# Joint wide and narrow attention: another filling order, another order of the last steps, and unit-matrix multiplications in the last four

## The chip, the core and the metric

The kernel runs on one core of a Trainium2 chip. The metric is the device time of one execution in microseconds, the median of three runs. A core has TensorE (PE: matrix products; its weight loads are shown as PEld), VectorE (DVE), ScalarE (ACT), GpSimd (POOL) and SyncE (SP), whose queue issues the DMAs here. Each engine takes its instructions in the order in which they were written and waits on semaphores.

## The reference

All of it is float32, on x of 32 batches, 128 tokens and 128 features, with a context of 128 tokens and 96 features for each batch. Five attention layers and two feed-forward layers follow one another; the change touches only the last two attention layers, which the kernel computes in one joint stage.

```python
# wide layer (L2): 16 heads of 64
h = layernorm(x, gamma, beta)
Q, K, V = h @ Wq, context @ Wk, context @ Wv          # 1024 columns each
attn = softmax(einsum('bihd,bjhd->bhij', Q, K), -1) * 64 ** -0.5
x = x + einsum('bhij,bjhd->bihd', attn, V).reshape(B, N, 1024) @ Wo + bo
# narrow layer (L3): 16 heads of 8, weights transposed in use
q, k, v = x @ Wq.T, context @ Wk.T, context @ Wv.T    # 128 columns each
attn = softmax(einsum('bhqd,bhkd->bhqk', q, k) * 8 ** -0.5, -1)
x = einsum('bhqk,bhkd->bhqd', attn, v).reshape(B, N, 128) @ Wo.T + bo + x
```

## The kernel before

The whole program is a row of stages with a barrier of all engines between them. The last stage, `wide_and_narrow`, starts at 1104.2 us of the profiled span and runs to its end. It is a software pipeline over the 32 batches: step t works on several batches at once, and each engine has its own list of what it does in a step (the loops `for t in range(first, last + 1)`, at the end of each engine's part). Steps run from -4 to 35. Operations of the wide layer begin with `w_`, those of the narrow one with `n_`.

The wide layer of batch b: statistics and mean (`w_statistics`, VectorE), one over the deviation and the normalised rows (`w_inverse_deviation`, `w_normalise`, GpSimd), a transposition (`w_transpose_h`, TensorE), scale and shift (`w_turned_h`, VectorE), queries in two halves (`w_queries`, eight instructions each), keys and values of two batches at a time in four quarters (`w_keys`, `w_values`; copied out by ScalarE, one quarter by VectorE), scores in two halves of eight heads (`w_score`), row maxima (VectorE), exponentials (ScalarE), sums, division (`w_divide`, GpSimd), and the turning of the probabilities in squares (`w_turn_squares`, VectorE) with two DMAs through device memory (`away`, `back`, on SP's queue). In step t TensorE makes the scores of batch t+1 first and weighs the values of batch t-1 after them. Until the first weighing, in step 1, most operations have nothing beside them: this is the filling, steps -4 to 0.

The narrow layer of batch b comes one step behind the wide one: transposition of x and projections in step b+1, then `n_set_parts` (GpSimd: six operations that lay keys and queries apart by groups of heads, so that four groups can use four row tiles of TensorE), scores whose maxima are taken (`n_score_for_max`, step b+2), the maxima turned and appended to the queries (`n_transpose_maxima`, `n_append_maxima`), scores less the maxima (`n_score_less_max`, step b+3, four groups in the order 2, 3, 0, 1), exponentials of each group, weighing (`n_weigh`, step b+4), turning back, division (`n_divide`), transposition (`n_transpose_o`), projection out and the sum with x (`n_finish`). After step 31 only the narrow layer is left but for the weighing of the last wide batch in step 32: in step 33 batch 31 has its scores for the maxima and batch 29 its weighing, in step 35 batch 31 its weighing and end.

PSUM has eight banks. Four hold scores: `scores[:, 0]` the wide scores' first half and the narrow scores for the maxima (`s_bank`), `scores[:, 1]` the second half and the narrow scores less the maxima (`t_bank`), two banks each, so groups 0 and 1 reuse the banks of groups 2 and 3. The other four are a ring that all other products go through; `Fills` lists them in the order of TensorE, and `start_fill` waits until the fill four places back was copied out.

`keep_clock` multiplies the unit matrix by itself a number of times; each is two instructions. The stage begins with ten of them.

Of the kernel before, what the change touches and what calls it, by code (L numbers as in the profile page):

```python
# [26 lines left out]
START_COUNT = 10  # L27
# [1287 lines left out]
def wide_and_narrow(nc, W, N, x, ctxT, ctx_blocks, ident, minus_half, eps, quad_mask, waits, store):  # L1315
# [8 lines left out]
             ("n.v", -3, "act"), ("n.Wo", -4, "dve"), ("n.mT", -2, "dve")]  # L1324
    first, last = -4, BATCHES + 3
    LAST_WIDE = BATCHES - 1
# [14 lines left out]
    def values_made(b):  # L1341
        return (b + 1) // 2 * 2 - 1

    ring = Fills((name, t + lag, engine) for t in range(first, last + 1)
                 for name, lag, engine in (turned_by_pe if t == LAST_WIDE + 1 else []) + order
                 if (makes_keys_values(t) if name.startswith("w.kv") else 0 <= t + lag < BATCHES))
    chunks = INNER // 128
# [9 lines left out]
    with ExitStack() as ctx:  # L1357
# [100 lines left out]

        def t_bank(g):
            return scores[:, 1, g % 2, :, :]  # L1460

        @block.tensor
        def _(pe):
            keep_clock(nc, scores[:, 0, 0, 0, :], ident, START_COUNT)
            for semaphore, value in waits:
# [8 lines left out]
            def filled_by(instruction, name):  # L1474
                instruction.then_inc(filled[ring.engine[name]], 1)

            def w_score(b, s):
# [37 lines left out]
            def n_score_less_max(b, g, j):  # L1515
                part = slice(QUAD * g, QUAD * (g + 1))
                if j == 0:
                    await_emptied(pe, "n.mT", b)
                    if g < 2:
                        pe.wait_ge(n_exp_ready, 4 * b + g + 1)  # L1520
                    elif real(b + 4):
                        pe.wait_ge(w_shifted, b + 5)
                    elif b >= 1:
                        pe.wait_ge(n_exp_ready, 4 * b - 3 + g)
                last = nc.tensor.matmul(t_bank(g)[:, j, :], n_k_apart[part, b % 2, j, :],  # L1525
                                        n_q_part[part, b % 2, j // 2, :],
                                        start=True, stop=True, tile_position=(QUAD * g, 0))
                if j == GROUP - 1:
                    last.then_inc(n_t_full, 1)
# [88 lines left out]

            def n_transpose_maxima(b):
                pe.wait_ge(n_max_ready, 4 * b + 4)  # L1620
                filled_by(nc.tensor.transpose(start_fill("n.mT", b)[:, 0:TOKENS],
                                              n_maxima[:, b % 2, :, :, :].rearrange("p g j d -> p (g j d)"),
                                              ident[:, :]), "n.mT")

            def n_weigh(b):
                pe.wait_ge(n_exp_ready, 4 * b + 4)
# [12 lines left out]

            def n_turn_back(b):  # L1640
                await_emptied(pe, "n.PV", b)
# [9 lines left out]

            def n_transpose_o(b):
                await_emptied(pe, "n.D", b)
                filled_by(nc.tensor.transpose(start_fill("n.oT", b)[:, 0:TOKENS],
                                              n_rows_o[:, :, :].rearrange("p h d -> p (h d)"), ident[:, :]), "n.oT")
# [12 lines left out]

            def n_project_out(b):
                await_emptied(pe, "n.oT", b)  # L1670
                filled_by(nc.tensor.matmul(start_fill("n.Wo", b)[:, 0:DIM], n_oT[:, :], N.wo[:, :],
                                           start=True, stop=True), "n.Wo")

            for t in range(first, last + 1):
                if t == LAST_WIDE + 1:
# [12 lines left out]
                if real(t - 1):  # L1688
                    w_project_out(t - 1)
                if real(t - 4):  # L1690
                    n_turn_back(t - 4)
                n_both_scores(t, (0, 1), (2, 3))
                if makes_keys_values(t):
                    if t % 2:
                        w_values(t)
                    else:
                        w_keys(t)
                n_both_scores(t, (2, 3), (0, 1))
                if real(t - 1):
# [17 lines left out]
        def _(act):  # L1717
# [25 lines left out]
            def n_exponentiate(b, g):  # L1743
                act.wait_ge(n_t_full, 4 * b + T_ORDER.index(g) + 1)
                nc.scalar.activation(n_exps[:, b % 2, GROUP * g:GROUP * (g + 1), :].rearrange("p h q -> p (h q)"),  # L1745
                                     t_bank(g).rearrange("p j q -> p (j q)"), ACT.Exp,
                                     scale=N.scale).then_inc(n_exp_ready, 1)
# [22 lines left out]
            def n_values(b):  # L1770
                if b == 0:
                    act.wait_ge(cleared, 3)
                copied("n.v", b, n_v[:, b % 2, :, :, 0:NARROW],
                       bank("n.v", b)[:, 0:DIM].rearrange("p (c e d) -> p c e d", e=2, d=NARROW))

            for t in range(first, last + 1):
                if t == LAST_WIDE + 1:
# [37 lines left out]
        def _(dve):  # L1815
            for semaphore, value in waits:
                dve.wait_ge(semaphore, value)
            nc.vector.memset(n_maxima[:, :, :, :, :], 0.0).then_inc(cleared, 1)
            nc.vector.memset(n_v[:, :, :, :, :], 0.0).then_inc(cleared, 1)
            dve.wait_ge(cleared, 2)  # L1820
            nc.vector.memset(n_v[:, :, :, :, NARROW:NARROW + 1], 1.0).then_inc(cleared, 1)

# [3 lines left out]
            def w_statistics(b):  # L1826
# [5 lines left out]
                nc.vector.memset(wait_carrier[:, :], 0.0)  # L1832
                nc.vector.bn_aggr(moments[:, p, :], stats[:, p, :]).then_inc(moments_ready, 1)

            def w_row_maxima(b, s):
# [58 lines left out]
            def n_append_maxima(b):  # L1894
# [5 lines left out]
                                               n_q_part[:, b % 2, 1, :], ALU.mult, ALU.add).then_inc(emptied["dve"], 1)  # L1900

            def n_divide(b):
                await_filled(dve, "n.D", b)
# [7 lines left out]
            def n_finish(b):  # L1911
# [3 lines left out]
                                        ALU.add).then_inc(emptied["dve"], 1)  # L1915

            for t in range(first, last + 1):
                if real(t + 1):
# [14 lines left out]
                if real(t - 1):  # L1933
                    w_finish(t - 1)
                if real(t - 4):
                    n_divide(t - 4)
                if real(t - 2):
                    n_find_maxima(t - 2, 0)
                    n_find_maxima(t - 2, 1)
                if real(t + 1) and t + 1 != LAST_WIDE:  # L1940
                    w_turn_squares(t + 1, 0)
# [9 lines left out]
                if real(t - 2):  # L1951
                    n_append_maxima(t - 2)

        @block.gpsimd
        def _(pool):
# [3 lines left out]
            def w_inverse_deviation(b):  # L1959
                p = b % 2  # L1960
                pool.wait_ge(moments_ready, b + 1)
                nc.gpsimd.tensor_tensor(var_eps[:, p, :], moments[:, p, 1:2], eps[:, :], ALU.add).then_inc(var_ready, 1)
                pool.wait_ge(var_ready, b + 1)
                nc.gpsimd.tensor_tensor(rstd[:, p, :], var_eps[:, p, :], minus_half[:, :],
                                        ALU.pow).then_inc(rstd_ready, 1)
# [27 lines left out]
            def n_set_parts(b):  # L1993
# [10 lines left out]
                done.then_inc(n_parts_ready, 1)  # L2004

            nc.gpsimd.memset(no_bias[:, :], 0.0).then_inc(masks_ready, 1)
            for n in range(2):
                nc.gpsimd.tensor_tensor(half_mask[:, n:n + 1], quad_mask[:, 2 * n:2 * n + 1],
                                        quad_mask[:, 2 * n + 1:2 * n + 2], ALU.add).then_inc(masks_ready, 1)
            pool.wait_ge(masks_ready, 3)  # L2010
            for t in range(first, last + 1):
                if real(t - 2):
                    n_set_parts(t - 2)
# [14 lines left out]
        def _(sp):  # L2028
# [10 lines left out]
            def back(b, h):  # L2039
# [4 lines left out]
                for j in range(SQUARES):  # L2044
                    sp.dma_start(w_probsT[SQUARE * j:SQUARE * (j + 1), b % 2, :, SLOT_HEADS * h:SLOT_HEADS * (h + 1), :],
                                 w_relay[h].rearrange("(i b) j h a -> j b i h a", b=SQUARE)[j]
                                 ).then_inc(w_probsT_landed[b % 2][h], 16)

            for t in range(first, last + 2):
                if real(t - 5):  # L2050
# [321 lines left out]
```

## Time and profile before

| | |
|---|---|
| runs | 1671.55 us median of 3 (1671.17 to 1672.45) |
| profiled execution: its time, its span | 1667.4 us, 1665.6 us |
| granted TensorE clock, mean over the span | 0.983 |
| busy over the span | PE 1599.6 us (96%), DVE 1201.9 (72%), ACT 1046.6 (63%), POOL 756.7 (45%) |
| joint stage | from 1104.2 us to the end |
| PE busy in 1120 to 1160 | 29.2 of 40 us |
| PE busy in 1202 to 1258 | 55.5 of 56 us |

The table is read so: in the middle of the stage TensorE hardly pauses, in its first 60 us it does. The granted clock is a share of full speed: 1.00 is 2.4 GHz, 0.50 is 1.2 GHz.

### The profile page before, as it was taken

What the parts mean: (1) busy time and instruction counts of PE and PEld (TensorE: products, weight loads), DVE (VectorE), ACT (ScalarE), POOL (GpSimd) and SP (SyncE); (2) the same over time, 40 slices, a digit from 0 to 9 for tenths busy, and PEclk for the clock granted to TensorE, in tenths of its full rate; (3) what the DMA queues carried; (4) which work ended last, traced back from release to release, by engine and by line L of the source; (5) the groups of instructions that cost most, each with busy time, mean ns of one, the idle gap of its engine ahead of it and who ended that gap; (6) DMA issues with size and microseconds to landing.
All of it is one profiled execution on the core that took longest, in us unless ns stands there. A gap on an engine that the chain in (4) does not pass through costs nothing. (4 is left out here: it accounts for less than half of the span.)

```text
span 1665.6 us, 49749 instructions
## 1 busy us (share of the span) xinstructions
PE 1599.6 (96%) x18240; PEld 1365.4 (82%) x18240; DVE 1201.9 (72%) x2395; ACT 1046.6 (63%) x3075; POOL 756.7 (45%) x1126
## 2 busy tenths in 40 slices
PE   7999999999999999989999998978999999999997
PEld 6888888878888888868978887867898898898986
DVE  5777777777777777746757775646887787888872
ACT  4777777777777777743336665435666666666663
POOL 3444444454444444422314442644555554555541
PEclk9999999999999999999999999998999999999997
DMA  7777667788677767740040000004545446444430
GB/s 198 197 196 188 184 184 200 201 210 217 185 187 192 188 185 192 190 140 9 0 115 2 3 3 2 1 1 127 154 137 166 145 136 178 124 141 146 135 117 9
DMA packets 229002, 220.07 MB, mean 132 GB/s; under 512 B 20610, under 2 KB 225092, under 8 KB 228740
## 3 DMA queue, kind: packets, MB, share of 16 engines
q1 hardware_dynamic: 228836, 217.79, 47.5%
q8 instruction: 112, 1.84, 0.5%
q14 instruction: 54, 0.44, 0.1%
HBM read 116.01 MB, written 101.71 MB: 131 GB/s over the span
## 5 line engine op out<-in xcount | busy, mean ns | idle before, releaser
L952 POOL TENSOR_TENSOR L_probs<-L_probs,L_inv_sum 128x1024 f32<-128x1024 f32 x128 | 242.8, 1897 | 88.3 <-DVE L_inv_sum L848 88.3
L736 ACT ACTIVATE L_probs<-L_scores,L_neg_max 128x128 f32<-128x128 f32 x512 | 182.7, 386 | 134.6 <-DVE L_neg_max L828 134.6
L822 DVE TENSOR_REDUCE L_row_max<-L_scores 128x8 f32<-128x1024 f32 x128 | 156.2, 1220 | 42.5 <-PE L_scores L594 42.5
L854 DVE STREAM_TRANSPOSE L_squares<-L_probs 128x1024 f32<-128x1024 f32 x125 | 153.0, 1224 | 0.3 <-POOL L_probs L952 0.3
L1983 POOL TENSOR_TENSOR L2L_w_probs<-L2L_w_probs,L2L_w_inv_sum 128x1024 f32<-128x1024 f32 x64 | 121.4, 1896 | 62.0 <-DVE L2L_w_inv_sum L1863 60.4
L1999 POOL TENSOR_SCALAR L2L_n_k_apart<-L2L_n_qk,quad_mask 128x128 f32<-128x128 f32 x128 | 55.5, 448 | 186.1 <-ACT L2L_n_qk L1724 175.8
L1735 ACT ACTIVATE L2L_w_probs<-L2L_scores,L2L_w_neg_max 128x128 f32<-128x128 f32 x256 | 91.2, 385 | 74.3 <-DVE L2L_w_neg_max L1843 74.3
L594 PE MATMUL L_scores<-L_kT,L_qT 64*128 64x128 f32 x2048 | 131.8, 278 | 0.9 <-ACT L_kT L725 0.9
L645 PE MATMUL L_ring<-L_probsT,L_v 128*64 128x128 f32 x2048 | 126.6, 276 | 4.7 <-issue 3.8
L645 PEld LDWEIGHTS L_ring<-L_probsT,L_v 128*64 128x64 f32 x2048 | 110.5, 137 | 24.7 <-issue 21.8
L594 PEld LDWEIGHTS L_scores<-L_kT,L_qT 64*128 64x128 f32 x2048 | 119.4, 188 | 12.5 <-ACT L_oT L725 8.1
L838 DVE TENSOR_REDUCE L_sums<-L_probs 128x8 f32<-128x1024 f32 x64 | 78.1, 1220 | 65.9 <-ACT L_probs L743 65.9
L1244 DVE TENSOR_REDUCE L_maxima<-L_s_banks 128x4 f32<-128x512 f32 x128 | 87.5, 688 | 43.5 <-PE L_s_banks L1066 43.5
L736 ACT ACTIVATION_READ_ACCUMULATOR L_probs<-L_scores,L_neg_max 128x1 f32 x512 | 115.7, 226 | 0.0
L725 ACT ACTIVATE L_oT<-L_ring 128x512 f32<-128x512 f32 x128 | 76.5, 599 | 40.5 <-PE L_ring L645 40.5
L1837 DVE TENSOR_REDUCE L2L_w_row_max<-L2L_scores 128x8 f32<-128x1024 f32 x64 | 76.8, 1199 | 28.6 <-PE L2L_scores L1494 28.6
L1745 ACT ACTIVATE L2L_n_exps<-L2L_scores 128x512 f32<-128x512 f32 x128 | 73.6, 605 | 37.8 <-PE L2L_scores L1525 37.7
L1891 DVE TENSOR_REDUCE L2L_n_maxima<-L2L_scores 128x4 f32<-128x512 f32 x128 | 82.3, 685 | 18.3 <-PE L2L_scores L1509 18.3
L1302 POOL TENSOR_SCALAR L_k_apart<-L_qk,quad_mask 128x128 f32<-128x128 f32 x116 | 50.3, 448 | 93.0 <-ACT L_qk L1202 93.0
L725 ACT ACTIVATE L_kT<-L_ring 128x512 f32<-128x512 f32 x128 | 76.8, 600 | 18.2 <-PE L_ring L602 18.2
L725 ACT ACTIVATE L_qT<-L_ring 128x512 f32<-128x512 f32 x128 | 76.2, 595 | 14.9 <-PE L_ring L602 9.5
L938 POOL TENSOR_TENSOR L_x_bias<-x,bias_L0a 128x128 f32<-128x128 f32 x32 | 14.6, 455 | 148.6 <-DVE x L870 148.6
(239 smaller groups left out, 4491.7 us busy)
## 6 DMA issues: line engine op xcount, KB each, us to landing
L_relay<-L_squares SPq DMA_DIRECT2D x125, 512.0 KB, 3.4
L_probsT<-L_relay SPq DMA_DIRECT2D x500, 128.0 KB, 3.7
L2L_relay<-L2L_w_squares SPq DMA_DIRECT2D x62, 512.0 KB, 3.6
L2L_w_probsT<-L2L_relay SPq DMA_DIRECT2D x248, 128.0 KB, 2.9
ctx_blocks<-ctx_turned SPq DMA_DIRECT2D x48, 128.0 KB, 3.5
out_x<-x SPq DMA_DIRECT2D x32, 64.0 KB, 2.8
ctx_turned<-ctxT SPq DMA_DIRECT2D x1, 1536.0 KB, 7.1
L0a_wq<-in_L_xattn_Wq SPq DMA_DIRECT2D x2, 256.0 KB, 3.1
```

The source lines that it names most:

```text
L594: last = nc.tensor.matmul(scores[:, s, r, i, :], q[part, i, at.n % 2, :], k[part, i, at.n % 2, :], start=True, stop=True, tile_position=(h ...
L645: last = nc.tensor.matmul(to[WIDE * r:WIDE * (r + 1), TOKENS * i:TOKENS * (i + 1)], v[:, at.n % 2, WIDE * h:WIDE * (h + 1)], probsT[:, at. ...
L725: nc.scalar.activation(to, src, ACT.Copy).then_inc(emptied["act"], 1)
L736: done = nc.scalar.activation(slot_probs(at, 0)[:, n, :], scores[:, 0, r, i, :], ACT.Exp, scale=layer_of(at).scale, bias=neg_max[:, n:n + ...
L822: nc.vector.tensor_reduce(row_max[:, s, :], slot(s), AX.X, ALU.max).then_inc(max_ready[s], 1)
L838: nc.vector.tensor_reduce(sums[:, :, 1, :], slot_probs(at, 1).rearrange("p (r i) k -> p r i k", r=2), AX.X, ALU.add).then_inc(sum_ready, 1)
L854: nc.vector.transpose(squares[:, at.n % 2, :, SLOT_HEADS * s:SLOT_HEADS * (s + 1), :] .rearrange("p j h a -> p h j a"), slot_probs(at, s). ...
L952: nc.gpsimd.tensor_tensor(to, to, inv_sum[:, :, s, :].unsqueeze(3) .to_broadcast([TOKENS, 2, GROUP, TOKENS]), ALU.mult).then_inc(divided, 1)
L1244: nc.vector.tensor_reduce(maxima[:, b % 2, g, :, 0:1].rearrange("p j d -> p (j d)"), s_bank(b, g), AX.X, ALU.max, negate=True).then_inc(ma ...
L1735: done = nc.scalar.activation(w_slot(b, 0)[:, h, :], scores[:, 0, r, i, :], ACT.Exp, scale=W.scale, bias=w_neg_max[:, h:h + 1], accum_out= ...
L1891: nc.vector.tensor_reduce(n_maxima[:, b % 2, g, :, 0:1].rearrange("p j d -> p (j d)"), s_bank(g), AX.X, ALU.max, negate=True).then_inc(n_m ...
L1983: nc.gpsimd.tensor_tensor(to, to, w_inv_sum[:, :, s, :].unsqueeze(3) .to_broadcast([TOKENS, 2, GROUP, TOKENS]), ALU.mult).then_inc(w_divid ...
```

## The change

The steps -4 to -1 are replaced by one written-out order on each engine, and the loops start at step 0. TensorE begins with the keys of batches 0 and 1, without the ten unit-matrix multiplications before; then it turns h of batches 0 and 1, makes the queries of batch 0, its scores, the queries of batch 1, turns h of batch 2 and makes the values of batch 0. The first three batches are normalised by VectorE, not GpSimd. VectorE's clearing of `n_maxima` and `n_v` (three memsets) moves from the stage's start to just before step 0. SP has the relay of batch 0's first half ahead of its loop. GpSimd's masks come after its first three deviations.

At the end: in step 32 VectorE, not GpSimd, sets the parts of batch 31, after it has appended the maxima of batch 30. In step 33 turning back batch 29 comes between the two blocks of scores, and its division after the maxima of the first two groups. In step 34 the scores less the maxima of batch 31 are made in one block of four groups, groups 0 and 1 in the banks of `scores[:, 0]`, and turning back batch 30 comes after them. In steps 33 to 35 `hold_clock` puts unit-matrix multiplications into a ring bank just before it is filled: 4, 3, 5 in step 33; 2, 3 in step 34; 4, 2, 3, 2 in step 35.

```diff
--- before.py
+++ after.py
@@ wide_and_narrow: fills of the ring, first step
-    first, last = -4, BATCHES + 3
+    first, last = 0, BATCHES + 3
+    DVE_NORMALISES = 3
+    kv = [(f"w.kv{g}", "dve" if g == 1 else "act") for g in QUARTERS]
+    filled_before = [*((name, -2, engine) for name, engine in kv), ("w.hT", 0, "dve"), ("w.hT", 1, "dve"),
+                     ("w.q0", 0, "act"), ("w.q1", 0, "act"), ("w.q0", 1, "act"), ("w.q1", 1, "act"),
+                     ("w.hT", 2, "dve"), *((name, -1, engine) for name, engine in kv)]
...
-        def t_bank(g):
-            return scores[:, 1, g % 2, :, :]
+        def t_bank(b, g):
+            return scores[:, 0 if b == BATCHES - 1 and g < 2 else 1, g % 2, :, :]
@@ TensorE
-            keep_clock(nc, scores[:, 0, 0, 0, :], ident, START_COUNT)
...
+            def hold_clock(name, b, count):
+
+                if b > LAST_WIDE - 3:
+                    keep_clock(nc, start_fill(name, b)[:, 0:TOKENS], ident, count)
...
@@ n_score_less_max
-                    if g < 2:
+                    if g < 2 and b == BATCHES - 1:
+                        pe.wait_ge(n_max_ready, 4 * b + 4)
+                    elif g < 2:
                         pe.wait_ge(n_exp_ready, 4 * b + g + 1)
...
+            def n_transpose_maxima: if b == LAST_WIDE: hold_clock("n.mT", b, 5)
+            def n_weigh:            if b == LAST_WIDE: hold_clock("n.PV", b, 4)
+            def n_turn_back:        if b == LAST_WIDE: hold_clock("n.D", b, 2)
+            def n_transpose_o:      hold_clock("n.oT", b, 3)
+            def n_project_out:      hold_clock("n.Wo", b, 2 if b == LAST_WIDE else 0)
...
@@ TensorE, ahead of the loop
+            w_keys(-2)
+            for b in range(2):
+                w_transpose_h(b)
+            for n in range(2):
+                w_queries(0, n)
+            for s in range(2):
+                w_score(0, s)
+            for n in range(2):
+                w_queries(1, n)
+            w_transpose_h(2)
+            w_values(-1)
             for t in range(first, last + 1):
...
-                if real(t - 4):
+                if real(t - 4) and t not in (LAST_WIDE + 2, LAST_WIDE + 3):
                     n_turn_back(t - 4)
-                n_both_scores(t, (0, 1), (2, 3))
+                if t == LAST_WIDE + 2:
+                    hold_clock("n.D", t - 4, 4)
+                if t == LAST_WIDE + 3:
+                    hold_clock("n.D", t - 4, 2)
+                    n_both_scores(t, (), (2, 3, 0, 1))
+                else:
+                    n_both_scores(t, (0, 1), (2, 3))
...
+                if t == LAST_WIDE + 2:
+                    n_turn_back(t - 4)
+                if t != LAST_WIDE + 3:
+                    n_both_scores(t, (2, 3), (0, 1))
+                if t == LAST_WIDE + 3:
+                    n_turn_back(t - 4)
@@ ScalarE, ahead of the loop
+            w_keys_values(-2, (0, 2, 3))
+            w_queries(0, 0)
+            w_queries(0, 1)
+            w_queries(1, 0)
+            w_exponentiate_0(0, 0)
+            w_queries(1, 1)
+            w_exponentiate_0(0, 1)
+            w_keys_values(-1, (0, 2, 3))
+            w_exponentiate_1(0)
@@ VectorE (the memsets are taken from its start)
+            def w_normalise(b):
+                dve.wait_ge(moments_ready, b + 1)
+                dve.wait_ge(rstd_ready, b + 1)
+                if b >= 1:
+                    await_filled(dve, "w.hT", b - 1)
+                nc.vector.tensor_scalar(w_rows_h[:, :], x[:, b, :], moments[:, b % 2, 0:1], rstd[:, b % 2, :],
+                                        ALU.subtract, ALU.mult).then_inc(w_rows_h_ready, 1)
...
+            w_statistics(0); w_statistics(1); w_normalise(0); w_keys_values(-2, 1); w_turned_h(0); w_normalise(1)
+            w_statistics(2); w_turned_h(1); w_row_maxima(0, 0); w_negate_maxima(0); w_row_maxima(0, 1)
+            w_subtract_maxima(0); w_normalise(2); w_turned_h(2); w_invert(0, 0); w_statistics(3)
+            w_keys_values(-1, 1); w_turn_squares(0, 0)
+            nc.vector.memset(n_maxima[:, :, :, :, :], 0.0).then_inc(cleared, 1)
+            nc.vector.memset(n_v[:, :, :, :, :], 0.0).then_inc(cleared, 1)
+            dve.wait_ge(cleared, 2)
+            nc.vector.memset(n_v[:, :, :, :, NARROW:NARROW + 1], 1.0).then_inc(cleared, 1)
...
-                if real(t - 4):
+                if real(t - 4) and t != LAST_WIDE + 2:
                     n_divide(t - 4)
                 if real(t - 2):
                     n_find_maxima(t - 2, 0)
                     n_find_maxima(t - 2, 1)
+                if t == LAST_WIDE + 2:
+                    n_divide(t - 4)
...
+                if t == LAST_WIDE + 1:
+                    n_set_last_parts()          # the six operations of n_set_parts(31)
@@ GpSimd
+                if b >= 2:
+                    pool.wait_ge(w_rows_h_ready, b - 1)     # in w_inverse_deviation
...
+            for b in range(DVE_NORMALISES):
+                w_inverse_deviation(b)
...
+            w_divide(0, 0)
+            w_inverse_deviation(3)
             for t in range(first, last + 1):
-                if real(t - 2):
+                if real(t - 2) and t - 2 != LAST_WIDE:
                     n_set_parts(t - 2)
@@ SP, ahead of the loop
+            away(0, 0)
+            back(0, 0)
```

## Rows read from the trace of the kernel before

**Rows 1.** Chain of waits, filling: start us, us, engine, what is written, line, count.
```profile
1104.94 1.34 DVE L2L_n_v L1819
...
1111.68 4.36 PE L2L_ring L1558 x46
1116.06 0.61 ACT L2L_w_kT L1724
...
1118.00 1.12 PE L2L_scores L1494 x16
1119.14 1.24 DVE L2L_w_row_max L1837
...
1120.61 2.91 ACT L2L_w_probs L1735 x16
...
1125.76 1.25 DVE L2L_w_squares L1869
...
1127.37 2.07 PE L2L_ring L1546 x8
...
1131.50 1.24 DVE L2L_w_row_max L1837
```

**Rows 2.** TensorE in order of time: start us, us, line, operation, count, [idle before].
```profile
1104.23 2.47 PE L157 MATMUL L2L_scores<-ident 128*128 128x128 f32 x20 [0.79 <-PEq L2116]
...
1116.94 1.07 PE L1546 MATMUL L2L_ring<-L2L_w_hT,L_wq 128*128 128x128 f32 x8
...
1136.49 2.87 PE L1558 MATMUL L2L_ring<-ctx_blocks,L_wk 32*128 32x256 f32 x48 [2.83 <-ACT L2L_w_qT L1724]
...
1639.51 1.08 PE L1633 MATMUL L2L_ring<-L2L_n_exps,L2L_n_v 128*32 128x128 f32 x32 [0.47 <-ACT L2L_n_v L1724]
```

**Rows 3.** Stretches, TensorE, filling: length, busy (count), granted clock, DMA share, GB/s.
```profile
1128.00:1129.00 1.00, 1.00 (x6) 0.50 0.73 251
```

**Rows 4.** VectorE's normalising in the feed-forward stage: ns min/median/max.
```profile
L2272 DVE TENSOR_SCALAR L1ff_rows_h<-y,L1ff_moments,L1ff_rstd x32: 339/468/614, 1036.3 to 1094.4; 128x128 f32 x20, 128x128 f32<-128x128 f32 x12
```

**Rows 5.** VectorE in order of time: parts in an earlier stage, appending in step 32.
```profile
849.53 1.11 DVE L1235 TENSOR_SCALAR L_k_apart<-L_qk,quad_mask 128x128 f32<-128x128 f32 x4 [3.11 <-ACT L_qk L1202]
850.56 0.60 DVE L1238 TENSOR_SCALAR L_q_part<-L_qk,L_half_mask,L_half_bias 128x128 f32<-128x128 f32 x2
...
1639.43 0.34 DVE L1899 SCALAR_TENSOR_TENSOR L2L_n_q_part<-L2L_ring,L2L_half_mask,L2L_n_q_part 128x128 f32<-128x128 f32 x1
```

**Rows 6.** Chain of waits, steps 32 to 35.
```profile
1635.19 1.05 PE L2L_scores L1509 x3
...
1637.15 0.27 PE L2L_ring L1650
...
1642.00 0.45 PE L2L_scores L1509
...
1643.91 1.25 PE L2L_scores L1509 x3
...
1646.78 0.40 PE L2L_ring L1654
...
1648.75 1.97 PE L2L_ring L1633 x32
...
1651.61 1.14 PE L2L_scores L1525 x16
...
1655.91 0.42 PE L2L_ring L1654
...
1657.88 1.97 PE L2L_ring L1633 x32
...
1663.34 0.29 DVE x L1914
```

**Rows 7.** Stretches, TensorE, step 33.
```profile
1643.00:1644.00 1.00, 0.61 (x11) 0.91 0.00 0
...
1645.00:1646.00 1.00, 1.00 (x19) 0.50 0.00 0
```

More of the change, by code:

```diff
@@ L1342, in values_made @@
         return (b + 1) // 2 * 2 - 1
-    ring = Fills((name, t + lag, engine) for t in range(first, last + 1)
-                 for name, lag, engine in (turned_by_pe if t == LAST_WIDE + 1 else []) + order
-                 if (makes_keys_values(t) if name.startswith("w.kv") else 0 <= t + lag < BATCHES))
+    ring = Fills(filled_before + [(name, t + lag, engine) for t in range(first, last + 1)
+                                  for name, lag, engine in (turned_by_pe if t == LAST_WIDE + 1 else []) + order
+                                  if (makes_keys_values(t) if name.startswith("w.kv") else 0 <= t + lag < BATCHES)])
     chunks = INNER // 128
@@ L1524, in n_score_less_max @@
                         pe.wait_ge(n_exp_ready, 4 * b - 3 + g)
-                last = nc.tensor.matmul(t_bank(g)[:, j, :], n_k_apart[part, b % 2, j, :],
+                last = nc.tensor.matmul(t_bank(b, g)[:, j, :], n_k_apart[part, b % 2, j, :],
                                         n_q_part[part, b % 2, j // 2, :],
@@ L1619, in n_transpose_maxima @@
             def n_transpose_maxima(b):
+                if b == LAST_WIDE:
+                    hold_clock("n.mT", b, 5)
                 pe.wait_ge(n_max_ready, 4 * b + 4)
@@ L1625, in n_weigh @@
             def n_weigh(b):
+                if b == LAST_WIDE:
+                    hold_clock("n.PV", b, 4)
                 pe.wait_ge(n_exp_ready, 4 * b + 4)
@@ L1640, in n_turn_back @@
             def n_turn_back(b):
+                if b == LAST_WIDE:
+                    hold_clock("n.D", b, 2)
                 await_emptied(pe, "n.PV", b)
@@ L1652, in n_transpose_o @@
             def n_transpose_o(b):
+                hold_clock("n.oT", b, 3)
                 await_emptied(pe, "n.D", b)
@@ L1669, in n_project_out @@
             def n_project_out(b):
+                hold_clock("n.Wo", b, 2 if b == LAST_WIDE else 0)
                 await_emptied(pe, "n.oT", b)
@@ L1697, in _ @@
                         w_keys(t)
-                n_both_scores(t, (2, 3), (0, 1))
+                if t == LAST_WIDE + 2:
[4 more added lines that the diff above has]
+                    n_turn_back(t - 4)
                 if real(t - 1):
@@ L1745, in n_exponentiate @@
                 nc.scalar.activation(n_exps[:, b % 2, GROUP * g:GROUP * (g + 1), :].rearrange("p h q -> p (h q)"),
-                                     t_bank(g).rearrange("p j q -> p (j q)"), ACT.Exp,
+                                     t_bank(b, g).rearrange("p j q -> p (j q)"), ACT.Exp,
                                      scale=N.scale).then_inc(n_exp_ready, 1)
@@ L1817, in _ @@
                 dve.wait_ge(semaphore, value)
[L1818 to L1821, printed above, removed]
             def slot_scores(s):
@@ L1900, in n_append_maxima, with n_set_last_parts @@
                                                n_q_part[:, b % 2, 1, :], ALU.mult, ALU.add).then_inc(emptied["dve"], 1)
+            def n_set_last_parts():
+                b = LAST_WIDE
+                await_emptied(dve, "n.qk", b)
+                dve.wait_ge(n_t_full, 4 * (b - 2) + 4)
+                dve.wait_ge(n_parts_ready, b)
+                for j in range(GROUP):
+                    other = (j + 2) % GROUP
+                    nc.vector.tensor_scalar(n_k_apart[:, b % 2, j, :], n_qk[:, b % 2, 1, :], quad_mask[:, j:j + 1],
+                                            quad_mask[:, other:other + 1], ALU.mult, ALU.add)
+                for n in range(2):
+                    done = nc.vector.tensor_scalar(n_q_part[:, b % 2, n, :], n_qk[:, b % 2, 0, :],
+                                                   half_mask[:, n:n + 1], no_bias[:, :], ALU.mult, ALU.add)
+                done.then_inc(n_parts_ready, 1)
             def n_divide(b):
@@ L1915, in n_finish @@
                                         ALU.add).then_inc(emptied["dve"], 1)
+            w_statistics(0)
+            w_statistics(1)
+            w_normalise(0)
+            w_keys_values(-2, 1)
+            w_turned_h(0)
+            w_normalise(1)
+            w_statistics(2)
+            w_turned_h(1)
+            w_row_maxima(0, 0)
+            w_negate_maxima(0)
+            w_row_maxima(0, 1)
+            w_subtract_maxima(0)
+            w_normalise(2)
+            w_turned_h(2)
+            w_invert(0, 0)
+            w_statistics(3)
+            w_keys_values(-1, 1)
+            w_turn_squares(0, 0)
+            nc.vector.memset(n_maxima[:, :, :, :, :], 0.0).then_inc(cleared, 1)
+            nc.vector.memset(n_v[:, :, :, :, :], 0.0).then_inc(cleared, 1)
+            dve.wait_ge(cleared, 2)
+            nc.vector.memset(n_v[:, :, :, :, NARROW:NARROW + 1], 1.0).then_inc(cleared, 1)
             for t in range(first, last + 1):
```

## Prediction

> **What bounds the kernel now.** I read the chain of waits over the first 70 us of the joint stage first, then the chain over the last 65 us, then the order of time on single engines for durations, and last the granted clock by the microsecond. In the first chain the reader is to see that no engine sets the pace before step 1: the chain jumps from VectorE to GpSimd to TensorE to ScalarE and back [rows 1]. From the stage's start at 1104.2 until VectorE begins the row maxima of batch 1 at 1131.50 it is 27.3 us, most of it one batch being handed from engine to engine. In the last chain the same is seen from 1639 on: parts from GpSimd, scores, maxima, exponentials, weighing, turning, projection, each waiting for the one before [rows 6]. Beside that, TensorE's granted clock is at the lower level, 1.2 GHz, in parts of both [rows 3, 7], and instructions there take nearly twice as long. Between the two lies the loop, which the diff leaves as it is from step 1 to step 31.
>
> The sum is made in the profiled execution: span 1665.6, its own time 1667.4, so 1.8 us lie around it. The median of the runs is 1671.55, 4.15 more; I take the difference in us over to that median unchanged.
>
> **The filling, step by step.** The first steps (-4 to -1) become one written-out order in which TensorE begins with the keys of batches 0 and 1 instead of ten multiplications of the unit matrix. The new chain, counted from 1104.2:
> - Keys: 48 instructions, 2.87 us at the full level [rows 2]; statistics, deviation and normalised rows of batch 0 fit beside them, since VectorE's first three memsets no longer stand ahead.
> - Copy of the first quarter 0.61 [rows 1], transposition of h 0.27 [rows 6], VectorE's scaling of it, then its normalising of batch 1 (which replaces GpSimd's), 0.47 each by the nearest row of that shape [rows 4], transposition 0.27.
> - Two sets of eight query products, 1.07 each [rows 2], and the first half of the scores, 1.12 [rows 1]. Seven hand-overs at 0.05: 0.35.
>
> Sum 2.87 + 0.61 + 0.27 + 0.94 + 0.27 + 2.14 + 1.12 + 0.35 = 8.6: row maxima of batch 0 at 1112.8, before 1119.14 [rows 1]; 6.3 gained. From there to the end of the first squares it is 7.87 before (1119.14 to 1125.76 + 1.25). Now ScalarE has the copy of the next queries ahead of the exponentials and another one between them. The first copy can begin only when TensorE has done the second half of the scores and eight queries, 1.12 + 1.07 after the maxima begin; with two copies (0.61) and the exponentials (2.91) they end at 2.19 + 0.61 + 2.91 + 0.61 = 6.3 instead of 4.4, so the squares end at 9.8. Then VectorE does the memsets, which before lay in an empty time and now stand ahead of the next row maxima: 1.34 for the large one [rows 1], and by its rate over the 288 columns of the others 0.25, so 1.6. Row maxima of batch 1: 8.6 + 9.8 + 1.6 = 20.0, at 1124.2 instead of 1131.50: **7.3 gained**. From here VectorE, ScalarE and GpSimd have the list of step 0 as before; the relay's first two DMAs are queued ahead of the loop on SP, in the order in which they were; nothing is moved past another queue. GpSimd's masks move behind three short deviations and are needed only by step 2. The added wait of a deviation for the normalised rows two batches back finds them done in the loop.
>
> Off that I take 1.0: the clock. In the filling before, eight queries took 2.07 at a granted 0.50 [rows 1, 3] against 1.07, and the new order has idle times of that kind too. I charge one set. Ends: none (7.3), or both sets, the half of the scores (1.12 more) and step 0's keys at 4.36 instead of 2.87 (both seen, [rows 1, 2]): 2.0 + 1.1 + 1.5 = 4.6, leaving 2.7. Taken: **6.3**.
>
> The Trainium skill, "TensorE: Matmul & The Clock Gate", Part 1, says that the lower level is the default and that activity lifts it; that speaks against dropping the ten multiplications. In this trace the twenty instructions of those ten took 2.47 at once after the barrier, the full pace, so the level was still up from the stage before [rows 2]. By the page alone the keys would take 4.36, and the filling would give 4.8.
>
> **The end.** The forecast has TensorE at the full level, since 25 multiplications of the unit matrix now stand in the waits; one is 2.47/10 = 0.25 [rows 2].
> - Parts of batch 31 by VectorE: it ends the appending at 1639.77, four and two operations take 1.63 [rows 5], so 1641.4. Four multiplications begin when weighing ends, 1640.59 [rows 2], and end at 1641.6. Scores at 1641.6 instead of 1642.00 [rows 6]: -0.4.
> - Turning back batch 29 moves between the two halves of the scores, and the division behind two maxima; both lie in the wait of 1.91 for maxima [rows 6]. 0 to 0.4; I take +0.1.
> - Second half at the full level: 1.96 (1635.19 to 1637.15) instead of 2.87 (1643.91 to 1646.78): -0.9 [rows 6].
> - From there to weighing batch 30, 1.97 before: three multiplications stand ahead of the transposition on which the copy and ScalarE's last two exponentials wait, +0.75; TensorE's short pieces at full pace, -0.4; five more lie beside the exponentials and outlast them by about 0.5. +0.8.
> - Weighing 1.08 instead of 1.97 [rows 2, 6], twice: -1.8.
> - Scores of batch 31, all four groups at once in other banks, so that no half waits for exponentials. Before, from weighing's end at 1650.72 to the transposition at 1655.91: 5.2 [rows 6]. Now two multiplications 0.5; 32 instructions, at the keys' 0.06 each 1.9 (ends: 1.14 if four groups run beside each other as two did [rows 6], 2.3 if not at all; the keys, four groups too, are nearest); turning back, two transpositions, 0.5; the division with three multiplications beside it 1.1, an estimate. 4.0: -1.2.
> - Then exponentials and weighing as before; four multiplications lie beside them. 0.
> - The tail, 3.78 before (1659.85 to 1663.63 [rows 6]): TensorE's pieces at full pace, -0.5 to -0.7; the seven multiplications lie beside copies and the division, 0 to 0.2. -0.5.
>
> Sum: -0.4 + 0.1 - 0.9 + 0.8 - 1.8 - 1.2 - 0.5 = **-3.9**. Together 6.3 + 3.9 = 10.2: 1671.55 - 10.2 = **1661.4**.
>
> **Rivals.**
> - *The level falls once at the end all the same.* The multiplications may be too few; before, TensorE was 61% busy just ahead of the fall to 0.50 and it came nevertheless [rows 7]. One low stretch after 1643.9 costs the second half 0.9, eight multiplications 0.25 each and a weighing 0.9: 3.8, the end's gain is gone: 1665.2. Against it: the multiplications fill up to 25 times 0.25, 6 us, of an engine that waited. 0.2.
> - *The filling is in the lower level throughout*, for the idle times around the transpositions: 2.7 from the filling, 3.9 from the end: 1665.0. For it: three low stretches there before; against it: the pieces on the chain stand close together. 0.1. A second place of the same page (Part 4) says that a transposition doesn't count as busy as a product does; it would make this one likelier, and no row here separates them.
> - *The filling's gain is given back by step 1*, which needs the first relayed probabilities and may find them late: 1671.55 - 3.9 = 1667.7. Against it: their squares keep their place in VectorE's list. 0.06.
> - *Slower: the multiplications at the lower level.* If the level stays down from 1643.9 to the last instruction, the 21 later ones cost 0.5 each, 10.5, of which waits hide some 3; four groups of scores at half pace add 0.5, neither weighing nor second half gets shorter, and the 0.4 of the parts stays: the end is 7.6 longer. With a filling that gives 2.7 the sum is 1676.5. It decides where the end's loss exceeds the filling's gain. Against it: between 1650.7 and 1654 the level came back by itself, the 16 score instructions took 1.14 [rows 6]. 0.04.
>
> **How the numbers follow.** The forecast has 0.6, its own range 1659 (no charge, scores in 1.14, a tail shorter by 0.5) to 1664. The range that should hold 8 in 10 reaches to the second and third case with their own spread, and 2 below the first, for the terms that I could only bound: 1657 to 1667. A measurement of this kernel tells 0.2%, 3.3 us, from no change; below 1668.2 is faster: the forecast and the next three cases but for a spread of 0.07 of them, 0.89; same 0.07; slower 0.04.
>
> **What would show it.** Right: keys as the first TensorE instructions of the stage in 2.9 us; row maxima of batch 1 some 20 to 21 us after the start; loop steps as long as before; granted clock 1.00 from 1639 (less the shift) to the end; 32 score instructions in one block of about 2 us; the last weighing 1.1. Wrong: 0.50 at the end beside unit matrix instructions of 0.4 and more; maxima of batch 1 later than 24 us; step 1 waiting for DMA.

## The result and the profile after

The changed kernel takes **1653.54 us** (median of 5 runs, 1650.38 to 1657.46), the kernel before beside it 1671.17 (5 runs, 1663.95 to 1672.45): a ratio of **0.9913, interval 0.9889 to 0.9936**, 14.5 us faster (10.7 to 18.6). The two medians lie 17.6 apart; two of the five runs of the kernel before took 1663.95 and 1664.42, so its median says little, and what follows goes by the ratio with its interval. The forecast was 1661.4 with a range of 1657 to 1667: the direction is right, the time lies 3.5 below the range.

The profiled execution took 1657.46 us, its span 1655.7, 9.9 less than before. TensorE is busy in 96% of it, as before; that says little, since the instructions of line 157, the unit matrix, count as busy too. The filling is read from the chain of waits. Changed kernel, start us, us, engine, what is written, line, count:

```profile
1106.80 2.92 PE L2L_ring L1569 x48
...
1114.81 1.24 DVE L2L_w_row_max L1891
...
1119.86 2.93 PE L2L_ring L1582 x22
...
1124.94 1.34 DVE L2L_n_v L2004
...
1126.35 1.20 DVE L2L_w_row_max L1891
...
1131.31 5.47 PE L2L_ring L1569 x46
...
1138.75 1.12 PE L2L_scores L1503 x16
1139.89 1.24 DVE L2L_w_row_max L1891
```

In this execution the stage starts at 1106.62 (1104.20 before). From there the row maxima of batch 0 are 8.2 us away (14.9 before, [rows 1]), those of batch 1 19.7 (27.3), and the negated maxima of batch 2, one step of the loop later, 34.5 (42.7). TensorE's clock in the filling of the same trace: length, busy (count), granted clock, DMA share, GB/s:

```profile
1120.00:1121.00 1.00, 1.00 (x12) 0.50 0.00 0
1133.00:1134.00 1.00, 1.00 (x12) 0.50 0.13 45
```

These are the values of batch 0 (2.93) and the keys of step 0 (5.47): the lower level, 1.2 GHz, did come, but not where the forecast charged it. The end, in the chain of waits of the changed kernel:

```profile
1634.60 1.08 PE L2L_ring L1648 x32
1635.68 1.09 PE L2L_ring L157 x8
1636.77 0.32 PE L2L_scores L1518
...
1638.61 1.05 PE L2L_scores L1518 x3
...
1640.56 0.86 PE L2L_ring L157 x6
...
1642.41 1.12 PE L2L_ring L157 x10
1643.63 1.01 PE L2L_ring L1648 x32
1644.64 0.64 PE L2L_ring L157 x4
1645.29 1.10 PE L2L_scores L1536 x32
...
1647.43 0.34 PE L2L_ring L1672
...
1649.53 1.01 PE L2L_ring L1648 x32
...
1653.38 0.29 DVE x L1982
```

From the weighing of batch 29 (first line) to the last sum it is 19.07 us, 24.12 before (1639.51 to 1663.63, [rows 2, 6]). Weighing (32 instructions) is 1.01 where it was 1.97 twice, and the granted clock is 1.00 to the end, where before it fell to 0.50 in step 33 [rows 7]:

```profile
1652.00:1653.00 1.00, 0.99 (x8) 1.00 0.00 0
```

So the two traces differ thus: to the maxima of batch 2 -8.2, from there to the weighing of batch 29 +0.8 (493.4 against 492.6), the end -5.1; the stage is 12.4 shorter (547.0 against 559.4). It started 2.4 later, in code that the diff doesn't touch; that leaves the 9.9 of the spans.

### The profile page after: what moved, and what is told of

It reads as the page before. It is cut to its first block and busy times, and to the rows that moved or that the text cites. A ratio compares the mean times of both kernels' runs of the same rounds, so it can differ in the third digit from the quotient of the medians.

```text
span 1655.7 us, 49853 instructions
## 1 busy us (share of the span) xinstructions
PE 1595.3 (96%) x18276; PEld 1363.4 (82%) x18276; DVE 1204.7 (73%) x2404; ACT 1047.7 (63%) x3075; POOL 754.1 (46%) x1117
## 5 line engine op out<-in xcount | busy, mean ns | idle before, releaser
L594 PEld LDWEIGHTS L_scores<-L_kT,L_qT 64*128 64x128 f32 x2048 | 119.4, 188 | 12.5 <-ACT L_oT L725 8.1
L1175 ACT ACTIVATE L_exps<-L_t_banks 128x512 f32<-128x512 f32 x128 | 69.4, 596 | 19.9 <-PE L_t_banks L1078 19.9
```

The costliest lines, as they stand in the source:

```text
L594: last = nc.tensor.matmul(scores[:, s, r, i, :], q[part, i, at.n % 2, :], k[part, i, at.n % 2, :], start=True, stop=True, tile_position=(h ...
```

## The experiments

Ratios stand against the kernel before in runs on the same chip (medians 1668.58, 1668.12 and 1668.43 in the three sets). Theory A says that the filling and the end each give their own part and the parts add. Its rivals are that the filling gives all, that the multiplications of the unit matrix carry the end, and that something beyond the first and last steps gives part of it (theory C of the first two expectations).

**The filling alone**: the order of the last steps, their banks, parts and multiplications as before.

```
-            return scores[:, 0 if b == BATCHES - 1 and g < 2 else 1, g % 2, :, :]
+            return scores[:, 1, g % 2, :, :]
...
-                    keep_clock(nc, start_fill(name, b)[:, 0:TOKENS], ident, count)
+                pass
```

> The filling alone: the last steps are those of the kernel before, without unit-matrix multiplications. Theory A (the change works by its two parts, which add; the filling term of the prediction was too small because a low clock was charged to it): row maxima of batch 1 start 19.6 us after the stage's start instead of 27.3, batch 2 33.1 instead of 41.4, the time is 8 us under the kernel before, and the end (from the negated maxima of batch 31 to the last sum) takes 60.7 us as before. Theory B (the prediction's own term): 6.3 us under it. Theory C (the timed gain of 14 to 17 us comes from something beyond the first and last steps): 10 us or more under it, with loop steps shorter than 15.65 us.

1658.39 us, 0.9932 (0.9908 to 0.9956): 11.3 us faster (7.3 to 15.4). That is more than the prediction's 6.3; between theory A (8) and theory C (10 or more) the time does not decide. The trace speaks against C: from the negated maxima of batch 2 to the weighing of batch 29 it takes 492.9, before 492.6, so the steps between are not shorter. The negated maxima of batch 2 come 34.4 after the start, as in the change; the end takes 25.5, longer than the 24.1 before. Its chain of waits there:

```profile
1631.77 1.80 PE L2L_ring L1645 x32
...
1644.26 2.06 PE L2L_scores L1533 x16
...
1647.04 2.53 PE L2L_scores L1533 x16
...
1651.53 1.97 PE L2L_ring L1645 x32
```

Two blocks of scores and a wait between them, all slow: 2.06 to 2.53 for 16, weighing 1.97.

**The end alone**: the kernel before with only the hunks of the last steps, and the same without the multiplications.

```
                 if b > LAST_WIDE - 3:
-                    keep_clock(nc, start_fill(name, b)[:, 0:TOKENS], ident, count)
+                    start_fill(name, b)
```

> The last steps alone, in the new order and with the unit-matrix multiplications; the filling is that of the kernel before. Theory A: granted clock 1.00 to the last instruction, the end takes 55.6 us instead of 60.7, the time is 5 us under the kernel before. Theory B (the prediction's own term): 3.9 us. Theory C (more than the two parts): 7 us or more. If the level falls once all the same: 1 us or less.

> The last steps in the new order without the unit-matrix multiplications, filling as before. If the multiplications are what keeps the level up: 0.50 appears after batch 31's first scores, second score block of step 33 near 2.9 us and at least one weighing near 1.9, the end takes 58 to 60 us and the time is 1 to 3 us under the kernel before. If the new order alone closes the waits enough: 1.00 to the end, and without 25 multiplications in the way the end takes 53 to 54 us, 6 to 7 us under it.

With them 1664.27 us, 0.9974 (0.9958 to 0.9989): 4.3 us faster (1.8 to 7.0). Without them 1662.91, 0.9968 (0.9952 to 0.9985). From the weighing of batch 29 to the end it is 19.07 and 18.66. Chain of waits of the kernel without them:

```profile
1646.30 1.11 PE L2L_ring L1644 x32
...
1653.86 1.08 PE L2L_ring L1644 x32
...
1659.15 1.97 PE L2L_ring L1644 x32
```

The level falls only just before the last weighing (1.97). So the end's gain is there without a single multiplication: the order gives it, and the rival that they carry the end falls. That the parts add fits: 11.3 + 4.3 = 15.6 against 14.5 (10.7 to 18.6) for the whole change and 13.9 (11.2 to 16.5) when it was measured again, below. The size of the end alone (1.8 to 7.0) is too uncertain to tell theory A's 5 from the prediction's 3.9.

**The change without the multiplications**, the edit of the last diff, in two sets.

> The whole change without its unit-matrix multiplications. If they are what keeps the level up and the parts add: 8 us from the filling and 1 to 3 from the end, 9 to 11 us under the kernel before, 2 to 4 us more than with them. If they cost more than they give: 14 us under it.

> The whole change without its unit-matrix multiplications, once more. If they neither give nor take time on the mean (19.07 us from the weighing of batch 29 to the last sum with them, 17.1 to 18.7 without, by where the level falls): 14 to 15 us under the kernel before, within its interval the same as with them. If the first run's 17.5 is a gain of its own: 17 or more.

1651.08 us, 0.9895 (0.9874 to 0.9916), and 1653.31, 0.9906 (0.9885 to 0.9926). **The change again**, unaltered:

> The changed kernel once more, beside the others of this call on the same chip. If the two parts add (8.3 us of filling and 5.1 us of end in the traces): 13.4 us under the kernel before; the prediction's sum: 10.2; the difference of the first medians: 17.6.

1653.81 us, 0.9917 (0.9901 to 0.9933). The intervals overlap; no gain from the multiplications can be seen. The traces say why. With them the end, from the weighing of batch 29 to the last sum, took 19.07 in all of four traces, at a granted 1.00. Without them it took 17.1 to 19.6 in six (18.4 on the mean): 17.1 where the level stayed up, more where it fell for a part.

**The memsets in a wait**: the change without the multiplications, and VectorE's three memsets brought forward, behind the scaling of h of batch 1, where it waits for the first scores.

```
             w_turned_h(1)
+            nc.vector.memset(n_maxima[:, :, :, :, :], 0.0).then_inc(cleared, 1)
+            nc.vector.memset(n_v[:, :, :, :, :], 0.0).then_inc(cleared, 1)
...
             w_row_maxima(0, 0)
```

> The whole change without unit-matrix multiplications at the end, and with VectorE's three memsets between scaling h of batch 1 and the first row maxima, where it waits 2.5 us for the first scores. If the memsets stand on the chain, as the prediction's sum has them (1.6 us): row maxima of batch 1 start 17.6 to 18.0 us after the stage's start instead of 19.6 to 19.8, step 1 follows 1.5 to 2 us earlier, and the time is 1.5 to 2 us under the run without the multiplications. Rival (another wait takes their place, the keys of step 0 or TensorE's lower level): step 1 starts less than 0.5 us earlier.

> The kernel without multiplications and with the memsets in VectorE's wait, once more. If the 2.9 us that its trace shows up to step 1 are its own: 16 to 18 us under the kernel before, 2 to 3 more than the run without multiplications in this call. If they are lost again behind step 1: the same as that run.

1652.99 us, 0.9908 (0.9887 to 0.9929), and 1649.91, 0.9891 (0.9874 to 0.9907). Chain of waits of the first:

```profile
1125.11 1.20 DVE L2L_w_row_max L1891
...
1137.74 1.24 DVE L2L_w_row_max L1891
...
1645.07 1.11 PE L2L_ring L1648 x32
```

From the negated maxima of batch 0 to those of batch 1 it is 9.5 and 9.3, in eight traces of the new filling without this edit 11.3 to 11.5. Between traces in which the values of batch 0 took the same (2.94: 9.5 against 11.5; 2.21: 9.3 against 11.3) the difference is 2.0: that is what the memsets cost the change. The stage takes 541.9 and 541.2 against 545.4 and 546.4 in the two traces of the kernel without multiplications, which differs by the memsets alone, and 547.0 and 545.7 in those of the change. By the times, the second run is 3.4 under the kernel without multiplications in the same set (1653.31), with intervals that overlap, and across the sets the ratios of the two kernels lie among each other (0.9908 and 0.9891 against 0.9895 and 0.9906). So what the memsets bring is seen in the traces and not settled by the times; 1649.91 is the lowest median of all runs, and both kernels beat the one before in every set.

**Multiplications in the filling**: the last kernel, with 4 ahead of a transposition and 12 ahead of the keys of step 0.

```
+            keep_clock(nc, start_fill("w.hT", 2)[:, 0:TOKENS], ident, 4)
             w_transpose_h(2)
...
+                        if t == 0:
+                            keep_clock(nc, start_fill("w.kv0", t)[:, 0:TOKENS], ident, 12)
```

> The kernel with the memsets in the wait, and 4 unit-matrix multiplications before h of batch 2 is turned and 12 before the keys of step 0. If the lower level in the filling costs time on the chain: values of batch 0 take 1.5 us instead of 2.94, keys of step 0 take 2.9 instead of 5.5, and step 1 starts 1 to 1.5 us earlier than with the memsets in the wait alone. If that low stretch is hidden behind VectorE's list: within 0.4 us of it.

1655.38 us, 0.9917 (0.9900 to 0.9934), no gain: 2.4 above the kernel without these multiplications in the same set, and the intervals overlap. TensorE in order of time in its trace (start us, us, line, operation, count, [idle before]):

```profile
1121.34 1.58 PE L1582 MATMUL L2L_ring<-L_wv,ctx_blocks 32*128 32x256 f32 x24 [0.59 <-DVE L2L_w_hT L1943]
...
1130.59 2.87 PE L1569 MATMUL L2L_ring<-ctx_blocks,L_wk 32*128 32x256 f32 x48 [1.92 <-ACT L2L_w_qT L1768]
...
1135.84 1.98 PE L1557 MATMUL L2L_ring<-L2L_w_hT,L_wq 128*128 128x128 f32 x8 [1.35 <-DVE L2L_w_kT L1939]
1137.75 2.83 PE L1503 MATMUL L2L_scores<-L2L_w_kT,L2L_w_qT 64*128 64x128 f32 x32
```

Values take 1.58 and keys 2.87, the full pace, and the low stretch comes a step later, in the queries and scores of step 1 (1.98 and 2.83), which lie on the chain. That the multiplications did this is not shown. Values take 1.58 without them too, in the traces of the change again and of the kernel without multiplications again; and in the second trace of the memsets in the wait, which has none of them, keys and queries of the same steps are:

```profile
1128.73 2.87 PE L1569 MATMUL L2L_ring<-ctx_blocks,L_wk 32*128 32x256 f32 x48 [3.00 <-ACT L2L_w_qT L1765]
...
1133.99 2.08 PE L1557 MATMUL L2L_ring<-L2L_w_hT,L_wq 128*128 128x128 f32 x8 [1.36 <-DVE L2L_w_kT L1936]
```

From the start to the negated maxima of batch 2 it is 32.9 with these multiplications, 31.6 and 32.9 with the same memsets and without them. Neither outcome that was named beforehand came: step 1 is not earlier, and where the level falls differs between executions of the same code.

**The ten multiplications at the start** put back into the change.

```
         def _(pe):
+            keep_clock(nc, scores[:, 0, 0, 0, :], ident, START_COUNT)
```

> The whole change with the ten multiplications of the unit matrix kept at the start of the stage. If the level is up from the stage before and they only stand ahead of the keys: keys start 2.3 us later and take 2.9 us as without them, the time is 2 us over the changed kernel. If the keys need them to have the level up in the filling (the rule that a clock is low by default): the level stays 1.00 through the queries and values and step 1 starts no later.

1656.34 us, 0.9929 (0.9914 to 0.9943), 2.5 above the change in the same set, with intervals that overlap. Chain of waits:

```profile
1106.51 2.47 PE L2L_scores L157 x20
1108.98 2.88 PE L2L_ring L1570 x48
...
1128.30 1.20 DVE L2L_w_row_max L1892
```

They take 2.47, and the keys behind them take the 2.9 that they take without them. The row maxima of batch 1 come 21.8 after the start of the stage, in the two traces of the change 19.7 and 19.6. They bought nothing.

**The last scores in two blocks**, and **the last parts by GpSimd**, each in the change without multiplications.

```
-                if t == LAST_WIDE + 3:
-                    hold_clock("n.D", t - 4, 2)
-                    n_both_scores(t, (), (2, 3, 0, 1))
-                else:
-                    n_both_scores(t, (0, 1), (2, 3))
+                n_both_scores(t, (0, 1), (2, 3))
```

> The whole change without unit-matrix multiplications, and step 34 as in the kernel before: the scores less the maxima of batch 31 in two blocks, groups 0 and 1 in the banks of groups 2 and 3. If the one block gives what the traces show (32 instructions in 1.10 us, no wait for exponentials): the two blocks take 1.14 and 1.1 to 2.4 us with 0.7 to 0.8 of waiting between, and from the weighing of batch 29 to the last sum it takes 1.5 to 2.5 us longer than the 17.1 (level up) to 18.1 (level down for a part) without multiplications. By the prediction's term (1.9 for the block): 0.7 to 1.7 us longer.

```
-                if t == LAST_WIDE + 1:
-                    n_set_last_parts()
...
-                if real(t - 2) and t - 2 != LAST_WIDE:
+                if real(t - 2):
```

> The whole change without unit-matrix multiplications, and the parts of batch 31 set by GpSimd. If the move to VectorE gives what the prediction has (0.4 to 0.6 us): first scores of step 33 start 2.5 us after the weighing of batch 29 starts, as in the kernel before, instead of 1.9 to 2.0. If turning back and the level decide there: no difference.

Two blocks: 1659.31 us, 0.9953 (0.9936 to 0.9971), 6.0 above the same kernel with one block (1653.31). Parts by GpSimd: 1656.21, 0.9931 (0.9910 to 0.9951), 2.9 above, and the intervals overlap. Chains of waits, first of the two blocks, then of the parts by GpSimd:

```profile
1640.65 2.06 PE L2L_scores L1534 x16
...
1643.43 2.53 PE L2L_scores L1534 x16
...
1648.08 1.97 PE L2L_ring L1646 x32
```

```profile
1629.90 1.12 PE L2L_ring L1648 x32
...
1632.45 0.47 PE L2L_scores L1518 x2
...
1646.63 1.97 PE L2L_ring L1648 x32
```

Two blocks with their wait take 5.31 (1640.65 to 1645.96) where one takes 1.10. Nearly half of that is the clock, by an estimate: at 1.14 for a block [rows 6] and the wait of 0.72 it would be 3.0, and this trace is at 0.50 from its weighing at 1637.54 (1.97) on. The expectation of 1.5 to 2.5 us more was missed: from the weighing of batch 29 to the end it is 24.9, against 19.6 in the kernel without multiplications again, whose level fell at the same place and came back before the weighing of batch 31 (1.11). So the one block is worth more than its wait, and what the order does for the level and what it does for the waits are not told apart. Parts by GpSimd start the scores 2.55 after weighing starts, by VectorE 1.91: 0.6 from the edit itself; the rest of its end, 22.55, is the lower level, which here came early and stayed (weighing 1.93 and 1.97). It came at the same place without the edit, in the trace just named; that the edit made it stay is not shown by one trace.

## Why the prediction was wrong

The mechanism was right: a shorter filling and a shorter end, and the two add. By the traces the two parts give 8.2 + 5.1 = 13.3, where the sum had 6.3 + 3.9 = 10.2. Two terms failed, the clock in the filling and the block of scores in the end, and beside them the base was off.

**The clock in the filling.** "Off that I take 1.0: the clock" is the step that failed, and not by the price of the lower level. Three sets of lines on the way from the row maxima of batch 1 to those of batch 2: the changed kernel in order of time, then the kernel with the last parts by GpSimd and the kernel before, each from the chain of waits.

```profile
1131.31 5.50 PE L1569 MATMUL L2L_ring<-ctx_blocks,L_wk 32*128 32x256 f32 x48 [5.17 <-ACT L2L_w_qT L1765]
...
1136.85 0.69 DVE L1936 COPY L2L_w_kT<-L2L_ring 128x512 f32<-128x512 f32 x1 [0.90 <-PE L2L_ring L1569]
...
1137.68 1.07 PE L1557 MATMUL L2L_ring<-L2L_w_hT,L_wq 128*128 128x128 f32 x8
```

```profile
1124.73 1.20 DVE L2L_w_row_max L1891
...
1129.70 4.35 PE L2L_ring L1569 x46
...
1137.25 1.24 DVE L2L_w_row_max L1891
```

```profile
1141.75 1.82 PE L2L_ring L1546 x8
1143.58 2.03 PE L2L_scores L1494 x16
...
1145.64 1.24 DVE L2L_w_row_max L1837
```

In the change the keys of step 0 took 5.50, more than any row before had shown, and VectorE stood idle for 0.90 until they were done; the way is 13.5 (1126.35 to 1139.89). In two traces in which they took 5.2, VectorE waited 0.60 and the way is 13.2; in two in which they took 4.4 it did not wait, and the way is 12.5. So some 1.0 us of the lower level came through to the change, the values of batch 0 (2.94 against 1.58) cost it 0.2 before that, and the rest lay beside VectorE's list (maxima, squares, memsets). The charge of 1.0 was near. What the sum left out is the other side: the kernel before takes 14.1 for the same way (1131.50 to 1145.64), because its own step 1 falls to the lower level: eight queries 1.82 and half of the scores 2.03, in the change 1.07 and 1.12. The prediction took that step over as equal ("have the list of step 0 as before") and charged the clock to the change alone. On this way the change therefore gained 0.6 where the sum has -1.0. How much it gains is partly luck: over seven traces of the new filling the negated maxima of batch 2 come 33.3 to 34.6 after the start, over three of the old one 42.7 to 43.6.

Step by step:

- **The filling to the row maxima of batch 0** (forecast 8.6 from the start): 8.2. **To those of batch 1** (20.0): 19.7. The sum of rows held. The memsets' 1.6 stood in it and was 2.0.
- **The clock** (-1.0): +0.6, as told above. With the 7.6 gained to the row maxima of batch 1 that makes the 8.2.
- **No multiplications at the start**: right. By the prediction's reading of the Trainium skill, "TensorE: Matmul & The Clock Gate", Part 1 (the lower level is the default, and activity lifts it), the keys would have taken 4.36. They took 2.92 at a granted 1.00: TensorE had been at work for the stage before until 0.9 us earlier, so the default did not arise.
- **Parts** (-0.4): -0.3. **Turning back and division moved** (+0.1): -0.1. **Second half** (-0.9): -0.9. **To weighing batch 30** (+0.8): +1.1. **Weighing twice** (-1.8): -1.9. **Tail** (-0.5): -0.65. All within 0.3.
- **Scores of batch 31 in one block** (-1.2): -2.4, 2.8 (1644.64 to 1647.43) instead of the forecast 4.0. This is the mis-sized term of the end. I took 1.9 for the 32 instructions, by the keys; they took 1.10, no more than 16 did before ([rows 6], 1.14): four groups take no longer than two. The lower end that I had written down was the right one, and the row of the same operation was nearer than the keys' row. The other 0.4 is the division with three multiplications beside it, an estimate of 1.1 that was 0.7.
- **The level at 1.00 to the end**: right, but no gain came of it. The prediction counts 25 multiplications; there are 28, and its terms name all of them, so the sum is not touched. Where the level stays up by itself the multiplications cost about 2: in the change they stand ahead of the copy (1640.56 to 1643.63, 3.07; without them 1.82) and ahead of the last scores (0.64). Where the falls came, they cost 1.0 to 2.5.
- **The loop as long as before**: 0.8 longer here; over all 14 traces it was 490 to 495 us, whatever the edit.

The rest is the base: the median of 1671.55 came from 3 runs, while 50 runs of the kernel before lie between 1660.06 and 1673.65, median 1668.5. Of the 7.9 us between 1661.4 and 1653.54 the base makes 3.0, the two parts 3.1 (13.3 less 10.2), and the last 1.8 lies within the spread of the runs. The bounds of the terms that I had written down reach a gain of 12.0 (no charge, 1.14 for the block), which is 1659.5 from the median shown; the range went 2 below the forecast's own, and held nothing for the base.

Of the rivals, "the level falls once at the end", "filling at the lower level throughout", "step 1 waits for DMA" and "multiplications at the lower level" none occurred.

## What to carry to other kernels

Where no engine sets the pace, as in a filling or an end, a new order is worth what the hand-overs between engines cost, and here it could be summed from rows within half a microsecond. The clock could not: its falls lay elsewhere in each execution, so a charge for it belongs only on instructions that the next engine waits for, and on both kernels, since the one before has falls of its own to lose. Multiplications to hold a clock are worth trying only against the same order without them: here they made the end the same length every time, at no less than the fall that they prevent costs on the mean. And a median of 3 runs is a poor base for a gain of one per cent.

## What the runs showed of the hardware beyond that

The same code ahead of the stage ends at different times: over the 14 traces the joint stage started between 1102.1 and 1108.8, in two traces of one and the same kernel (no multiplications) at 1104.2 and 1107.8. That spread is larger than the end's whole gain. What sets it stays open.

A DMA of the same size lands later in some executions. Probabilities coming back through the relay in step 31, chain of waits of the changed kernel, then of the end alone with multiplications:

```profile
1607.61 3.05 DMA L2L_w_probsT<-L2L_relay
```

```profile
1610.54 4.22 DMA L2L_w_probsT<-L2L_relay
```

In 11 of the 14 traces this last read lands after 3.03 to 3.06 us, in three (the end alone with and without multiplications, and the multiplications in the filling) after 4.2 to 4.3. From the negated maxima of batch 31 to the weighing of batch 29 the eleven take 36.5 to 37.0 us, the three 37.7 to 39.3. No run took the late landing away to see the other, so that it is the cause is not shown, nor what makes it late.
